# A fused attention and feed-forward layer: the weighted sums of four heads issued in two bursts instead of five units

## The chip, the cores and the metric

One core of one Trainium2 chip. The metric is the device time of one execution in microseconds (us), as the median of several runs. The kernel works in float32, except for the score products, whose operands are split into three bfloat16 levels each.

## What is computed

For 8 batches of 512 tokens with 128 features: attention with 16 heads of width 8, added to the input and normalised, then a feed-forward part with a shift by one token, added and normalised again. Cut to what matters:

```python
raw = einsum('bhid,bhjd->bhij', q, k)
scores = alpha * tanh(raw / beta) + lam * hamming + lat      # two rank-6 biases, made from x
scores = where(causal, scores, -inf)
attn = softmax(scores)
out = einsum('bhij,bhjd->bhid', attn, v) @ out_w.T
x = layernorm(x + out)
x = layernorm(x + sigmoid(xr @ W_r.T) * (square(relu(xk @ W_k.T)) @ W_v.T))
```

## The kernel before, in words

The scores of a head are kept transposed, keys on the partitions and queries along the free side. Keys come in four blocks of 128 (jb 0 to 3), and block jb needs only the queries from 128·jb on, because of the causal mask. Four heads make a **quad**; its 16 blocks are packed into 5 **pairs** of two 512-wide banks: pairs 0 and 1 of a quad hold block 0 of two heads each, pairs 2 and 3 hold blocks 1 and 3 (384 and 128 wide) of two heads each, pair 4 holds block 2 (256 wide) of all four. So a batch is 4 quads, or 20 pairs (`PAIRS`), and the whole kernel is a pipeline over pairs.

A pair t goes through the engines like this. TensorE makes the products q·k into one of three PSUM slots (`scores`, tile `raw<-q_stack,k_stack`), and a slot is free again when VectorE has read it. ScalarE takes the tanh (L783, `raw` to `probs`). TensorE overwrites the slot with the biases (`biases`, `raw<-i_stack,j_stack`). VectorE adds both (`main`, L1004). ScalarE takes the exponential in place (L788), GpSimd zeroes the masked triangle (`mask`, L892), and TensorE multiplies by the values into the single PSUM bank `sums` (`weighted`). `probs` has ten pair buffers, and tanh of a pair waits until the weighted sums of the pair ten earlier have been counted by `pv_done`. Two quads accumulate in `sums`; then VectorE copies it out (`sums_out`, L1067) before the next quad may start.

All engines run one list of **steps**, t = 0 to 19 for each batch b, in program order, with fixed lags: in step t TensorE issues biases of pair t-1 and scores of pair t+1, ScalarE tanh of pair t and exp of pair t-3, VectorE `main` of t-1, GpSimd the mask of t-3. Beside them each step carries **side work** from fixed tables. Before attention of a batch can start its operands are prepared two batches ahead ("prep" for b+2), after it its output is finished one batch behind ("post" for b-1):

- TensorE: the tables `PREP_UNITS`, `VALUES_UNITS`, `POST_UNITS`. Every such unit writes the one PSUM bank `side_bank`, and each waits until the unit before it was read (`Side.before`). Prep: xT2 (transposes), q2, k2, F2, G2 (projections). Values: v1. Post: oT0, oT1 (transposes of `sums_sb`), aT, y, x1T, kk, rr, kv.
- VectorE: `PREP` and `POST`. Splitting a 512-wide float32 matrix into three bfloat16 levels alternates between engines: `hi` (VectorE, L1038), `rest` (GpSimd, L899), `mid` (VectorE, L1043), `lo` (GpSimd, L905). `mid` waits for `rest` of the same matrix (Q, K, J or G), and `rest` waits for `hi`. `values_in` (L1055) copies v1 out of `side_bank`. `residual` (L1101), `stats` (L1089) and `moments` (L1096) follow the unit y.
- GpSimd: `PREP` and `POST`: `inv_std` (L913, L915) and `norm` (L923, L927) make the normalised x1, which the unit x1T transposes.
- ScalarE: F2, kk and rr are read there (L796; L798 with L804; L800).

SyncE writes the levels to DRAM and loads them back as stacks (`q_stack`, `k_stack`, `i_stack`, `j_stack`) for the batch after.

`VALUES_STEPS` gives each of the 20 weighted units its step; a step of 20 or more is step minus 20 of the next batch. Unit p of a quad is: p = 0 and 1 the two halves (256 wide) of block 0, p = 2 block 1 (384), p = 3 block 3 (128), p = 4 block 2 (256); each is four products, one per head, in four column groups of the array. `AHEAD_FIRST` names the steps in which TensorE issues the scores of t+1 before the side units rather than last. Inside a step of TensorE the order is biases, (scores), side units, weighted sums left from the batch before, weighted sums of this batch, (scores).

Batch 0 has no post work; batches 1 to 5 have both; batch 6 has no prep but v1; batch 7 has neither, and a tail follows in which the last weighted sums and the last post work run by themselves.

Of the kernel before, what the change touches and what calls it, by code (L numbers as in the profile page):

```python
# [42 lines left out]
P = 128  # L43
# [18 lines left out]
VALUES_STEPS = [6, 7, 7, 9, 11, 11, 12, 13, 14, 15, 16, 18, 19, 19, 19, 20, 20, 24, 25, 25]  # L62
# [6 lines left out]
VALUES_UNITS = {7: ["v1"]}  # L69
POST_UNITS = {1: ["oT0"], 6: ["oT1"], 8: ["aT"], 10: ["y"], 14: ["x1T"], 16: ["kk"], 17: ["rr"], 18: ["kv"]}  # L70
# [69 lines left out]
def build(nc, x, qkv_w, out_w, hex_w, lam_logit, q6_w, transforms, transform_weights, scale_logit,  # L140
# [17 lines left out]
    with ExitStack() as ctx:  # L158
# [350 lines left out]
        def _(pe):  # L509
# [47 lines left out]
            def weighted(b, par, t):  # L557


                quad, p = divmod(t, PAIRS_PER_QUAD)  # L560
                k, s = divmod(quad, 2)

                pe.wait_ge(mask_done, PAIRS * b + last_of_group(t) + 1)
                if t == 0:
                    pe.wait_ge(dve_freed, side_units.made(b, "v"))
                if t == PAIRS // 2 or (t == 0 and not (isinstance(b, int) and b == 0)):
                    pe.wait_ge(sums_read, 2 * b + k)
                first_pair = last_of_group(t) - (1 if p < 4 else 0)

                def head(r, a, z):  # L570

                    return pair_probs(first_pair + (r // 2 if p < 4 else 0))[:, r % 2 if p < 4 else r // 2, a:z]


                jb, first, cols_of = [
                    (0, 0, lambda r: head(r, 0, T // 2)), (0, T // 2, lambda r: head(r, T // 2, T)),
                    (1, P, lambda r: head(r, 0, 3 * P)), (3, 3 * P, lambda r: head(r, 3 * P, T)),
                    (2, 2 * P, lambda r: head(r, (r % 2) * 2 * P, (r % 2 + 1) * 2 * P))][p]
                for r in range(4):
                    rhs = cols_of(r)  # L580
                    last = mm(sums[32 * r:32 * r + 32, first:first + rhs.shape[-1]],
                              values[par][:, jb, 4 * quad + r, :], rhs, start=(s == 0 and p == 0),
                              stop=(s == 1 and p == PAIRS_PER_QUAD - 1), skip_group_check=True)
                last.then_inc(pv_done, 1)
# [67 lines left out]
            def values_of(b, par, step):  # L652

                for t in range(PAIRS):
                    if VALUES_STEPS[t] == step:
                        weighted(b, par, t)
# [703 lines left out]
```

## Time and profile before

| | |
|---|---|
| median of 3 runs | 427.74 us (426.52 to 428.01) |
| the profiled execution | 426.69 us, span 424.7 us |
| TensorE products busy | 368.2 us, 87% |
| VectorE busy | 328.3 us, 77% |
| ScalarE busy | 327.3 us, 77% |
| GpSimd busy | 230.1 us, 54% |
| tanh and exp (L783, L788) | 160 each, mean 1025 and 1060 ns |
| main (L1004) | 160, mean 1273 ns |
| mean granted TensorE clock | 0.949 of full |

Busy time counts from start to end of each instruction; neighbours on one engine overlap by some hundredths of a microsecond, so that the distance from start to start is a little shorter than the duration. A product in float32 leaves two records in the trace, so four heads of one weighted unit are 8 records (1280 in all for 640 products). In the timeline, a number in brackets is the time for which the engine sat idle before, and what ended it.

### The profile page before, as it was taken

Reading aid. Unit: us, or ns where it says so; the run is one execution under the profiler, and the core shown is the slowest. Engines: PE = TensorE matmul, PEld = TensorE weight load, DVE = VectorE, ACT = ScalarE, POOL = GpSimd, SP = SyncE. Lnnn points to the kernel's source line nnn. Section 1 sums busy time; section 2 is a strip of 40 time slices with the busy share of each in tenths; the row PEclk is TensorE's granted clock in tenths of the full one; section 3 lists DMA queues with packets and bytes.
Section 4 is the critical chain, followed back from the end, with each engine's and each line's share of the span. In section 5 each row is a group of like instructions: output and inputs, shape, how many; then the busy total and the mean of one; then the engine's idle time right before and its main releaser. Section 6 shows DMA issues by size and latency. Waiting matters only on the chain.

```text
span 424.7 us, 8760 instructions
## 1 busy us (share of the span) xinstructions
PE 368.2 (87%) x2907; PEld 190.1 (45%) x2907; DVE 328.3 (77%) x539; ACT 327.3 (77%) x364; POOL 230.1 (54%) x367
## 2 busy tenths in 40 slices
PE   3557688899999999999899989999999998999863
PEld 1132233345455444645464446444544454345453
DVE  4874668987978788778978897879878867696643
ACT  1102398998998988798889899898889998999621
POOL 4313535823687449633975388645873446344631
PEclk9955899999999999999999999999999999899958
DMA  3254587786622774166634763376318620100000
GB/s 97 87 152 119 157 261 195 215 230 175 197 91 59 192 198 160 48 176 183 173 88 120 188 185 106 90 187 185 114 50 208 165 79 1 51 26 1 2 26 25
DMA packets 37807, 53.74 MB, mean 127 GB/s; under 512 B 3522, under 2 KB 35266, under 8 KB 36190
## 3 DMA queue, kind: packets, MB, share of 16 engines
q1 hardware_dynamic: 34078, 51.49, 43.4%
q10 hardware_dynamic: 3696, 1.84, 1.7%
q8 instruction: 18, 0.29, 0.3%
q14 instruction: 15, 0.12, 0.1%
HBM read 38.69 MB, written 14.61 MB: 126 GB/s over the span
## 4 chain that ended last, share of the span: by engine, by line
PE 43%; DVE 19%; issue 11%; POOL 10%; SPq 7%; ACT 5%; DMA 3%; ACTq 1%; DVEq 0%; POOLq 0%
PE raw L511 17%; PE side_bank L511 13%; PE sums L511 10%; DVE probs L1004 9%; ACT probs L788 3%; POOL probs L892 2%; ACT probs L783 2%; SPq L401 2%; PE side_bank L598 2%; POOL x L927 2%; POOL x L923 2%; SPq L415 2%; POOL parts L905 2%; SPq L412 2%; DVE bn L1089 1%
## 5 line engine op out<-in xcount | busy, mean ns | idle before, releaser
L1004 DVE SCALAR_TENSOR_TENSOR probs<-probs,scal,raw 128x1024 f32<-128x1024 f32 x160 | 202.3, 1273 | 32.5 <-PE raw L511 32.0
L783 ACT ACTIVATE probs<-raw 128x1024 f32<-128x1024 f32 x160 | 163.9, 1025 | 38.4 <-PE raw L511 37.7
L892 POOL TENSOR_SCALAR_AFFINE_SELECT probs<-probs 128x256 f32<-128x256 f32 (+1 forms) x224 | 98.5, 457 | 137.3 <-ACT probs L788 136.8
L788 ACT ACTIVATE probs<-probs 128x1024 f32<-128x1024 f32 x160 | 169.3, 1060 | 0.9 <-DVE probs L1004 0.9
L511 PE MATMUL raw<-q_stack,k_stack 72*128 72x384 bf16 (+3 forms) x512 | 98.2, 304 | 17.3 <-DVE probs L1004 13.6
L511 PE MATMUL raw<-i_stack,j_stack 111*128 111x384 bf16 (+3 forms) x512 | 97.2, 302 | 2.4 <-ACT probs L783 2.3
L511 PE MATMUL sums<-probs,values 128*32 128x256 f32 (+2 forms) x1280 | 93.4, 392 | 4.2 <-POOL probs L892 4.0
L511 PEld LDWEIGHTS raw<-q_stack,k_stack 72*128 72x128 bf16 x512 | 38.1, 98 | 71.4 <-DVE probs L1004 46.9
L511 PEld LDWEIGHTS raw<-i_stack,j_stack 111*128 111x128 bf16 x512 | 42.2, 98 | 47.4 <-issue 16.9
L511 PEld LDWEIGHTS sums<-probs,values 128*32 128x32 f32 x1280 | 29.7, 109 | 50.0 <-issue 26.1
L899 POOL TENSOR_TENSOR whole<-whole,parts 128x512 f32<-128x512 f32 x22 | 26.1, 1188 | 23.5 <-DVE parts L1038 23.5
L905 POOL TENSOR_TENSOR parts<-whole,parts 128x512 bf16<-128x512 f32 x30 | 35.1, 1170 | 4.2 <-DVE parts L1043 4.2
L1067 DVE COPY sums_sb<-sums 128x512 f32<-128x512 f32 x15 | 10.4, 692 | 20.0 <-PE sums L511 20.0
L1043 DVE CAST parts<-whole 128x512 bf16<-128x512 f32 x32 | 16.7, 522 | 2.9 <-POOL whole L899 2.8
L915 POOL TENSOR_TENSOR rstd<-var_eps,minus_half 128x4 f32<-128x4 f32 x14 | 14.6, 1046 | 1.2
L796 ACT ACTIVATE feats<-side_bank 128x512 f32<-128x512 f32 x8 | 4.9, 612 | 12.4 <-PE side_bank L511 12.4
L511 PEld LDWEIGHTS side_bank<-w_r_mix,x1T 128*128 128x128 f32 x112 | 13.6, 191 | 1.0
L511 PE MATMUL side_bank<-w_r_mix,x1T 128*128 128x128 f32 x112 | 13.6, 275 | 0.0
L1038 DVE CAST parts<-whole 128x512 bf16<-128x512 f32 x24 | 11.9, 498 | 1.8 <-DMA q_rows<-parts 1.6
L511 PE MATMUL side_bank<-x1T,w_k_mix 128*128 128x512 f32 x28 | 13.2, 591 | 0.0
L835 ACT ACTIVATE probs<-shift_col 1x1536 bf16<-1x1536 bf16 x1 | 1.5, 1481 | 14.6 <-DVE w_r_mix L1244 14.6
L1089 DVE BATCH_NORM_STATS2 bn<-res 128x6 f32<-128x128 f32 x56 | 12.2, 280 | 0.2
(144 smaller groups left out, 346.4 us busy)
## 6 DMA issues: line engine op xcount, KB each, us to landing
q_stack<-q_rows SPq DMA_DIRECT2D x21, 384.0 KB
k_stack<-k_rows SPq DMA_DIRECT2D x21, 384.0 KB
i_stack<-lattice_i SPq DMA_DIRECT2D x21, 288.0 KB
i_stack<-hamming_i SPq DMA_DIRECT2D x21, 288.0 KB
q_rows<-parts SPq DMA_DIRECT2D x8, 384.0 KB, 8.5
k_rows<-parts SPq DMA_DIRECT2D x8, 384.0 KB, 2.6
lattice_i<-parts SPq DMA_DIRECT2D x8, 288.0 KB
k_rows<-parts SPq DMA_DIRECT2D x8, 256.0 KB, 3.0
```

Of the source, the lines that this page charges most:

```text
L511: return nc.tensor.matmul(o, lhsT, rhs, start=start, stop=stop, **kw)
L783: nc.scalar.activation(pair_probs(t), raw[:, t % PSUM_PAIRS, :].rearrange("p (u i) -> p u i", u=2), ACT.Tanh).then_inc(tanh_done, 1)
L788: nc.scalar.activation(pair_probs(t), pair_probs(t), ACT.Exp).then_inc(exp_done, 1)
L892: last = nc.gpsimd.affine_select(out=v, in_=v, compare_op=ALU.is_ge, fill=0.0, base=0, pattern=[[0, v.shape[1]], [1, P]], channel_multipli ...
L899: nc.gpsimd.tensor_tensor(whole[:, kind, :], feats[:] if kind == J else whole[:, kind, :], parts[:, kind, 0, :], ALU.subtract).then_inc(re ...
L905: nc.gpsimd.tensor_tensor(parts[:, kind, 2, :], whole[:, kind, :], parts[:, kind, 1, :], ALU.subtract).then_inc(lo_done[kind], 1)
L915: nc.gpsimd.tensor_tensor(rstd[:], var_eps[:], minus_half[:], ALU.pow).then_inc(rstd_done, 1)
L1004: v.scalar_tensor_tensor(out=o, in0=o, scalar=scal[:, 2:3], in1=raw[:, t % PSUM_PAIRS, :].rearrange("p (u i) -> p u i", u=2), op0=ALU.mult ...
L1038: v.tensor_copy(parts[:, kind, 0, :], feats[:] if kind == J else whole[:, kind, :]).then_inc(hi_done[kind], 1)
L1043: v.tensor_copy(parts[:, kind, 1, :], whole[:, kind, :]).then_inc(mid_done[kind], 1)
L1067: v.tensor_copy(sums_sb[:, k, :], sums[:]).then_inc(sums_read, 1)
L1089: v.bn_stats(bn[:, blk, :], res[:, blk, :]).then_inc(bn_done, 1)
```

## The change

The five weighted units of a quad become two bursts. Part 0 multiplies block 0 of the four heads in full width (512) when pairs 0 and 1 are masked, and counts 2 on `pv_done`; part 1 multiplies blocks 1, 3 and 2 when all five pairs are masked, and counts 3. The steps are (6, 9), (11, 14), (16, 19), (21, 24), so 8 bursts per batch in place of 14 groups of adjacent units. The unit v1 and `values_in` move from step 7 to 11. The unit y, `residual`, `stats` and `moments` of the first normalisation move from 10 to 9, GpSimd's `inv_std` from 10 to 9 and its `norm` from 11 to 10. The unit kk (and ScalarE's part) moves from 16 to 15. On VectorE `hi` of Q moves from 5 to 4, `mid` of Q from 9 to 8, `hi` of K from 9 to 10, and `sums_out` comes after `main` of its step instead of ahead of it (in steps 5 and 15).

```diff
-VALUES_STEPS = [6, 7, 7, 9, 11, 11, 12, 13, 14, 15, 16, 18, 19, 19, 19, 20, 20, 24, 25, 25]
+VALUES_STEPS = [(6, 9), (11, 14), (16, 19), (21, 24)]
-VALUES_UNITS = {7: ["v1"]}
-POST_UNITS = {1: ["oT0"], 6: ["oT1"], 8: ["aT"], 10: ["y"], 14: ["x1T"], 16: ["kk"], 17: ["rr"], 18: ["kv"]}
+VALUES_UNITS = {11: ["v1"]}
+POST_UNITS = {1: ["oT0"], 6: ["oT1"], 8: ["aT"], 9: ["y"], 14: ["x1T"], 15: ["kk"], 17: ["rr"], 18: ["kv"]}
...
-            def weighted(b, par, t):
+            def weighted(b, par, quad, part):
+                pairs = (2, 3)[part]
+                pe.wait_ge(mask_done, PAIRS * b + first_pair + (2 if part == 0 else PAIRS_PER_QUAD))
...
+                blocks = [[(0, lambda r: head(r // 2, r % 2, 0, T))],
+                          [(1, lambda r: head(2 + r // 2, r % 2, 0, 3 * P)),
+                           (3, lambda r: head(2 + r // 2, r % 2, 3 * P, T)),
+                           (2, lambda r: head(4, r // 2, (r % 2) * 2 * P, (r % 2 + 1) * 2 * P))]][part]
+                for jb, cols_of in blocks:
+                    for r in range(4):
+                        last = mm(sums[32 * r:32 * r + 32, jb * P:T], values[par][:, jb, 4 * quad + r, :], cols_of(r),
+                                  start=(s == 0 and part == 0), stop=(s == 1 and jb == 2), skip_group_check=True)
+                last.then_inc(pv_done, pairs)
...
 (GpSimd)
-            POST = {10: [(inv_std, 0)], 11: [(norm, 0)], 18: [(gated_residual,)], 19: [(inv_std, 1), (norm, 1)]}
+            POST = {9: [(inv_std, 0)], 10: [(norm, 0)], 18: [(gated_residual,)], 19: [(inv_std, 1), (norm, 1)]}
...
 (VectorE)
-            PREP = {0: [(x_out,)], 2: [(projected, Q)], 3: [(projected, K)], 5: [(hi, Q)], 9: [(mid, Q), (hi, K)],
+            PREP = {0: [(x_out,)], 2: [(projected, Q)], 3: [(projected, K)], 4: [(hi, Q)], 8: [(mid, Q)], 10: [(hi, K)],
                     11: [(mid, K), (hi, J)], 12: [(features_i,)], 13: [(hi, G)], 15: [(mid, J)], 17: [(mid, G)]}
-                    10: [(residual,), (stats, 0, 0), (stats, 0, 1), (moments, 0)], 14: [(x1_out,)],
+                    9: [(residual,), (stats, 0, 0), (stats, 0, 1), (moments, 0)], 14: [(x1_out,)],
...
-                    if t == VALUES_STEPS[-1] - PAIRS and post:
-                        sums_out(b - 1, 1)
-                    if t == VALUES_STEPS[PAIRS // 2 - 1]:
-                        sums_out(b, 0)
                     if t >= BIAS_LAG or post:
                         main(*lagged(b, t, BIAS_LAG))
+                    if t - 1 == VALUES_STEPS[-1][1] - PAIRS and post:
+                        sums_out(b - 1, 1)
+                    if t - 1 == VALUES_STEPS[QUADS // 2 - 1][1]:
+                        sums_out(b, 0)
```

## Rows read from the trace of the kernel before

**Rows 1.** Busy us of PE, PEld, DVE, ACT, POOL; clock, DMA share, GB/s: one period.

```profile
181.80:227.20 45.40, 43.09 (x362) 22.60 (x360) 38.47 (x61) 40.25 (x45) 28.68 (x45) 1.00 0.53 145
```

**Rows 2.** Waits from 181.8 to 227.2 us: total, times, longest (us).

```profile
ACT probs L783 <- PE raw L511: 4.9, 8, 1.5
...
DVE sums_sb L1067 <- PE sums L511: 2.7, 2, 2.0
```

**Rows 3.** Timeline, ScalarE: tanh of pair 2 in batches 3 and 4.

```profile
181.41 1.01 ACT L783 ACTIVATE probs<-raw 128x1024 f32<-128x1024 f32 x1
...
226.82 1.02 ACT L783 ACTIVATE probs<-raw 128x1024 f32<-128x1024 f32 x1
```

**Rows 4.** Timeline, TensorE: groups of weighted units and what came next.

```profile
200.81 1.07 PE L511 MATMUL sums<-probs,values 128*32 128x256 f32 x16
...
201.81 0.61 PE L511 MATMUL raw<-q_stack,k_stack 72*128 72x384 bf16 x4
...
220.38 1.50 PE L511 MATMUL sums<-probs,values 128*32 128x384 f32 x24
...
221.83 0.60 PE L511 MATMUL raw<-q_stack,k_stack 72*128 72x512 bf16 x2
```

**Rows 5.** Timeline, VectorE: the copy of the sums in step 5.

```profile
189.13 0.69 DVE L1067 COPY sums_sb<-sums 128x512 f32<-128x512 f32 x1 [2.00 <-PE sums L511]
```

**Rows 6.** Timeline, steps 7 to 13 of batch 3: side work and the tanh of pair 13.

```profile
194.52 0.76 DVE L1055 COPY values<-side_bank 128x256 f32<-128x256 f32 x2
...
198.95 1.06 PE L511 MATMUL side_bank<-woT,attnT 128*128 128x128 f32 x8
...
201.34 0.68 DVE L1101 TENSOR_TENSOR res<-side_bank,x_res 128x512 f32<-128x512 f32 x1
...
201.88 1.17 POOL L905 TENSOR_TENSOR parts<-whole,parts 128x512 bf16<-128x512 f32 x1
...
202.69 1.02 PE L511 MATMUL side_bank<-feats,lat_map 128*128 128x512 f32 x2
...
203.00 1.17 POOL L899 TENSOR_TENSOR whole<-whole,parts 128x512 f32<-128x512 f32 x1
203.07 0.38 DVE L1096 BATCH_NORM_AGGREGATE mean_var<-bn 128x2 f32<-128x6 f32 x4 [0.15 <-DVE bn L1089]
...
203.37 1.26 DVE L1004 SCALAR_TENSOR_TENSOR probs<-probs,scal,raw 128x1024 f32<-128x1024 f32 x1
...
203.64 0.64 PE L511 MATMUL sums<-probs,values 128*32 128x256 f32 x8
204.14 0.23 POOL L913 TENSOR_SCALAR var_eps<-mean_var 128x4 f32<-128x4 f32 x1
204.44 1.05 POOL L915 TENSOR_TENSOR rstd<-var_eps,minus_half 128x4 f32<-128x4 f32 x1
204.55 0.42 DVE L1043 CAST parts<-whole 128x512 bf16<-128x512 f32 x1
...
205.33 1.02 ACT L783 ACTIVATE probs<-raw 128x1024 f32<-128x1024 f32 x1 [0.63 <-PE raw L511]
205.46 0.77 POOL L892 TENSOR_SCALAR_AFFINE_SELECT probs<-probs 128x256 f32<-128x256 f32 x2
```

**Rows 7.** Busy time by stretch, 364 to 366 us, batch 7, and the same columns.

```profile
364.00:366.00 2.00, 2.00 (x12) 0.59 (x12) 1.01 (x1) 2.00 (x3) 0.42 (x2) 0.51 0.03 8
```

**Rows 8.** Timeline, ScalarE and TensorE: tanh of pairs 4 to 6 of batches 6 and 7.

```profile
321.29 1.03 ACT L783 ACTIVATE probs<-raw 128x1024 f32<-128x1024 f32 x1
...
324.99 1.05 ACT L783 ACTIVATE probs<-raw 128x1024 f32<-128x1024 f32 x1
...
363.85 1.03 ACT L783 ACTIVATE probs<-raw 128x1024 f32<-128x1024 f32 x1
...
368.35 1.02 ACT L783 ACTIVATE probs<-raw 128x1024 f32<-128x1024 f32 x1 [0.66 <-PE raw L511]
```

**Rows 9.** Timeline, TensorE: the last weighted unit of the kernel.

```profile
401.94 0.64 PE L511 MATMUL sums<-probs,values 128*32 128x256 f32 x8 [0.76 <-POOL probs L892]
```

More of the change, by code:

```diff
@@ L555, in biases @@
                 last.then_inc(bias_ready, 1)
-            def weighted(b, par, t):
-                quad, p = divmod(t, PAIRS_PER_QUAD)
+            def weighted(b, par, quad, part):
                 k, s = divmod(quad, 2)
-                pe.wait_ge(mask_done, PAIRS * b + last_of_group(t) + 1)
-                if t == 0:
+                first_pair = PAIRS_PER_QUAD * quad
+                pairs = (2, 3)[part]
+                pe.wait_ge(mask_done, PAIRS * b + first_pair + (2 if part == 0 else PAIRS_PER_QUAD))
+                if quad == 0 and part == 0:
@@ L565, in weighted @@
                     pe.wait_ge(dve_freed, side_units.made(b, "v"))
-                if t == PAIRS // 2 or (t == 0 and not (isinstance(b, int) and b == 0)):
+                if s == 0 and part == 0 and not (quad == 0 and isinstance(b, int) and b == 0):
                     pe.wait_ge(sums_read, 2 * b + k)
-                first_pair = last_of_group(t) - (1 if p < 4 else 0)
-                def head(r, a, z):
-                    return pair_probs(first_pair + (r // 2 if p < 4 else 0))[:, r % 2 if p < 4 else r // 2, a:z]
@@ L575, in weighted @@
[L575 to L583, printed above, removed]
@@ L584, in weighted, with head @@
-                last.then_inc(pv_done, 1)
+                def head(pair, unit, a, z):
+                    return pair_probs(first_pair + pair)[:, unit, a:z]
+                blocks = [[(0, lambda r: head(r // 2, r % 2, 0, T))],
[6 more added lines that the diff above has]
+                                  start=(s == 0 and part == 0), stop=(s == 1 and jb == 2), skip_group_check=True)
@@ L652, in values_of @@
             def values_of(b, par, step):
-                for t in range(PAIRS):
-                    if VALUES_STEPS[t] == step:
-                        weighted(b, par, t)
+                for quad, steps in enumerate(VALUES_STEPS):
+                    if step in steps:
+                        weighted(b, par, quad, steps.index(step))
             parity = [1]
@@ L738, in _ @@
                        range(JB)).then_inc(tail["first_sums_T"], 1)
-            for step in range(PAIRS, VALUES_STEPS[-1] + 1):
+            for step in range(PAIRS, VALUES_STEPS[-1][1] + 1):
                 values_of(B - 1, 1, step)
```

## The prediction, made before the changed kernel was run

> **What bounds the kernel now.** I read the page first, then busy time by stretch, the waits of one period, and the timeline step by step. One batch in the steady state is a period of 45.4 us, from one tanh of pair 2 to the next [rows 3]. No engine fills it: in that stretch TensorE is busy 43.1 us, ScalarE 40.3 and VectorE 38.5 [rows 1]. All three hand the same pair on, so the period is the work of ScalarE plus the time for which it waits for scores. That wait is 4.9 us in 8 places, at most 1.5 in one [rows 2]; some 40.5 us is the floor. Every side task is to be judged by whether it makes a tanh start later. The profiled execution has 426.69 us, 1.05 below the median of 427.74; I sum differences and add them to the median.
>
> **The change part by part.**
>
> *Bursts.* Two units of 256 take 1.00 us to the start of what follows, three of 384, 128 and 256 together take 1.45 [rows 4]. So 256 columns cost 0.45 and each burst about 0.1 more. Entering a burst is not seen apart; I bound both sides together by 0.1 and 0.25 us. Per batch 6 of 14 entries go: 0.6 to 1.5 us of TensorE. The 512-wide product is in no row; the nearest is the 1.00 for the same columns, which I take, between 0.9 and 1.1. What this gives by itself is nothing unless TensorE is what a tanh waits for; it also makes each remaining block longer (1.45 us), and what is queued behind it, the biases or scores of the next pair, waits for that. The Trainium skill (TensorEngine Tiling (Array Packing), Key Properties) says that changing the tiling mode drains the engine, which speaks for the change; the rows agree in that a burst costs more than its columns. By that rule alone each batch would gain its 1.5 us.
>
> *Copies of the sums.* Before, VectorE stood 2.0 us ahead of the copy in step 5, `main` of pair 4 behind it [rows 5], of 2.7 us in a period [rows 2]. Afterwards `main` goes first. `main` is no longer held, but the copy ends later, and oT1 waits for it on TensorE, with the first burst and the scores of pair 7 queued behind.
>
> *Steps 4 to 9.* I walked the queues from tanh of pair 2 at 181.41, with scores or biases 0.44 us apart, 0.64 from a product group's start to its reader, exp 0.91 after tanh and the next tanh 0.94 after exp (estimates from neighbours in the timeline). The burst in step 4 ends at 187.5, `main` of pair 4 runs from 188.1 to 189.4, the copy to 190.0, oT1 at 190.0, the first burst from 190.6 to 191.6. Tanh of pair 6 keeps its place, that of pair 7 is 0.4 late. Without v1 and two units in step 7, tanh of pair 9 comes at 196.0, 1.2 us earlier than before. y can start at 196.2, when aT has been copied (before: 198.95 [rows 6]); residual follows 1.06 later at 197.3, and moments end at 199.4, where they ended at 203.45 before [rows 6].
>
> *Steps 10 to 12, the term that decides.* Let m be the end of moments. GpSimd stands at `inv_std` in step 9, so in its queue follow inv_std 1.32 (204.14 to 205.46), the mask of pair 7 0.77, lo of Q 1.12 and rest of K 1.17 [rows 6], with about 0.2 to wake: rest of K is done at m + 4.6. Before, lo and rest ran while the moments were being made and inv_std stood behind them, so `mid` of K found its input ready. VectorE after m has `main` of 9 and 10 (1.18 each, 203.37 to 204.55) and hi of K (0.4 to 0.6): it is at `mid` of K at m + 2.9 and stops for 1.7 us. Behind that stop are mid of K and hi of J (0.33 each), and now values_in (0.76), which used to be in step 7 [rows 6]: done at m + 6.1. TensorE's G2 may not write the bank before v1 is out of it, G2 takes 0.95 (202.69 to 203.64), and in step 12 the scores of pair 13 stand behind G2: tanh of pair 13 at m + 7.7, 207.1 to 207.2. Before: 205.33 [rows 6]. TensorE stands 2.6 us ahead of G2. Loss at this point: 1.8 us, where without the stop it would be 0.1. Ends for the stop: nothing, if y or moments come so late that GpSimd does lo and rest first in effect; 2.6, all of TensorE's wait.
>
> *Steps 13 to 2.* The norm ends 2 us earlier than it did but now x1T no longer is what is late. kk in step 15 has x1T ready; ScalarE's relu and square come one pair earlier, same work. mid, hi and gate keep their places relative to the pair. The burst of quad 3 moves from step 0 to step 1 of the next batch, from ahead of scores 1 to ahead of scores 2; scores 1 waits for `main` of 19 anyway, which stands behind the second statistics. So the burst, hidden under that wait before, now costs: 0.5 us, against savings of about 0.6 before it. The walk ends with tanh of pair 2 at 228.5 against 226.82 [rows 3]: a period of 47.1, +1.7.
>
> *The sum.* Five periods have prep and post: 5 x 1.7 = 8.5. Batch 6 has no mid of K, but v1 and a burst in step 11 and the burst in step 1: +1.1 by the same walk. Batch 0 has no moments; its hi of Q, a step earlier, waits for the same transfer with `main` of 4 behind it, won back by step 9: +0.7 with its end. Batch 7: 0. Tail: after the last mask came one unit of 256, 0.64 [rows 9]; now comes the whole part 1, 1.49 in all: +0.85. Together 11.1, less rounding 11.0: 427.7 + 11.0 = **438.7 us**.
>
> *SyncE* gets its levels in the same order, some 2 us later for Q and K; their readers are a batch away, so nothing. Masks wait at most for inv_std; the earliest reader of a late one is the burst in step 14, done with it 2 us ahead. `pv_done` comes in lumps, three or more steps ahead of the tanh that needs it: nothing.
>
> **Rivals.** (a) *Faster: TensorE's entries are what bounds.* If TensorE's queue is the limit, 1.5 us go for each of 7.5 batches: 416.5. For it: 43.1 busy of 45.4, and 2.7 us of VectorE's waits that vanish. Against it: the walk finds G2 waiting for a copy, not for TensorE. It decides if rest of K is done by m + 2.9. Chance 0.18, spread from 415 to 425.
> (b) *No change.* The stop is there but covered: tanh of pairs 11 and 12 late from other causes, so that 13 loses nothing more, as the walk without the stop has it. 427 to 429. Chance 0.12.
> (c) *Slower still, by the clock.* In 364 to 366 the granted clock was 0.51, the level of 1.2 GHz [rows 7], after a sparse stretch of TensorE; tanh 4 to tanh 6 took 4.50 us there against 3.70 in batch 6 [rows 8]. A stop of 2.6 us ahead of G2 in five periods could call it each time: 5 x 0.8 = 4 more, 443. The Trainium skill (TensorE: Matmul & The Clock Gate, What's actually happening) says that the throttled state is the default and activity releases it; by that the gap could only harm. Against it: gaps of 0.4 to 1 us in the steady periods left the clock at 1.00 [rows 1]. Chance 0.12.
>
> **How the numbers follow.** Forecast 0.58 (433 to 441.5). A measurement tells about 0.5% from no change, so same is 425.6 to 429.9. Slower 0.70 (forecast and c), same 0.12, faster 0.18. The range from 427 to 444 leaves out rival (a), nearly all of it, and a little above. The likeliest case alone: 433 to 441.5, from the stop's 1.2 to 2.0 us in five periods and the burst's 0.1 us in 56 bursts.
>
> **What would show it.** Tanh of pair 2 some 47 us apart; five idle times of 1.2 to 2 us of VectorE ahead of L1043, ended by GpSimd's L899; TensorE waiting over 2 us for VectorE's L1055 ahead of the unit G2; ScalarE's wait for scores grown from 4.9 to nearly 7 us a period; the 2.0 us ahead of L1067 gone. If L1043 shows no such wait, or tanh of pair 13 comes within 24.5 us of that of pair 2 (before 23.9), I am wrong at steps 10 to 12. If the wait is there and the period has not grown, I am wrong in what it costs.

## The result, and the profile of the changed kernel

| | before | changed |
|---|---|---|
| median on one chip | 427.16 us (4 runs) | 467.38 us (4 runs, 465.01 to 469.01) |
| ratio | | 1.0926, 95% interval 1.0876 to 1.0975 |
| the profiled execution | 426.69 us, span 424.7 us | 467.9 us, span 466.0 us |
| TensorE's mean granted clock | 0.949 | 0.932 |

Medians are over all runs of a kernel; ratios leave out those more than 1.5% above its fastest (four of ten in e14, three of ten in e15, none elsewhere).

The sign of the forecast was right and its size was not: 40 us were lost, not 11, and the time lies above the range. The first look is at the busy time of the page of the changed kernel, since it tells whether work was added or waiting.

```profile
PE 378.4 (81%) x2651; PEld 196.6 (42%) x2651; DVE 344.4 (74%) x539; ACT 327.5 (70%) x364; POOL 230.3 (49%) x367
```

ScalarE and GpSimd work as long as before (327 and 230 us), so on them the 41 us of span are waiting. TensorE has 256 product records less but 10 us more busy time, and VectorE 16 us more with the same number of instructions: something makes single instructions longer. The groups by line name which (busy us, mean ns | idle time before them and what ended it).

```profile
L781 ACT ACTIVATE probs<-raw 128x1024 f32<-128x1024 f32 x160 | 163.6, 1023 | 77.1 <-PE raw L511 76.4
...
L1041 DVE CAST parts<-whole 128x512 bf16<-128x512 f32 x32 | 25.6, 800 | 10.6 <-POOL whole L897 10.4
L511 PE MATMUL side_bank<-feats,lat_map 128*128 128x512 f32 x16 | 15.3, 1056 | 23.8 <-DVE values L1053 22.6
```

The same groups before the change:

```profile
L783 ACT ACTIVATE probs<-raw 128x1024 f32<-128x1024 f32 x160 | 163.9, 1025 | 38.4 <-PE raw L511 37.7
...
L1043 DVE CAST parts<-whole 128x512 bf16<-128x512 f32 x32 | 16.7, 522 | 2.9 <-POOL whole L899 2.8
L511 PE MATMUL side_bank<-feats,lat_map 128*128 128x512 f32 x16 | 10.1, 720 | 1.2 <-DVE lat_map L1198 1.2
```

Line numbers in this region have gone down by two. ScalarE's wait for scores went from 37.7 to 76.4 us: those 38.7 us are nearly the whole loss, on the engine that hands every pair on. G2 waits 22.6 us for `values_in` where it waited for nothing, and `mid` waits 10.4 us for `rest` (before 2.8); both waits were forecast. Not forecast are the means: the cast of `mid` went from 522 to 800 ns, G2 from 720 to 1056 ns.

One period, from the tanh of pair 2 in batch 3 to that in batch 4, is 52.08 us where [rows 1] and [rows 3] have 45.4. Its stretch (same columns as [rows 1]) and then its waits:

```profile
198.91:250.99 52.08, 45.06 (x339) 23.91 (x338) 42.84 (x62) 42.23 (x47) 29.23 (x45) 0.97 0.47 127
```

```profile
ACT probs L781 <- PE raw L511: 11.5, 8, 5.5
...
PE side_bank L511 <- DVE values L1053: 4.3, 1, 4.3
...
DVE parts L1041 <- POOL whole L897: 1.9, 1, 1.9
```

The number of waits for scores is still 8, as in [rows 2], but one of them alone has 5.5 us, more than all eight together in [rows 2]. The timeline of steps 10 to 13 of batch 3 shows how it is built; it answers to [rows 6].

```profile
216.89 0.38 DVE L1094 BATCH_NORM_AGGREGATE mean_var<-bn 128x2 f32<-128x6 f32 x4 [0.15 <-DVE bn L1087]
...
218.36 0.42 DVE L1036 CAST parts<-whole 128x512 bf16<-128x512 f32 x1
...
220.65 1.15 POOL L897 TENSOR_TENSOR whole<-whole,parts 128x512 f32<-128x512 f32 x1
...
221.76 1.04 POOL L921 TENSOR_TENSOR x<-res,mean_var 128x512 f32<-128x512 f32 x1
221.84 1.25 DVE L1041 CAST parts<-whole 128x512 bf16<-128x512 f32 x1 [1.87 <-POOL whole L897]
222.95 1.04 POOL L925 TENSOR_TENSOR x<-x,rstd 128x512 f32<-128x512 f32 x1
223.01 1.26 DVE L1036 CAST parts<-feats 128x512 bf16<-128x512 f32 x1
...
224.19 0.74 DVE L1053 COPY values<-side_bank 128x256 f32<-128x256 f32 x2
...
224.99 1.90 PE L511 MATMUL side_bank<-feats,lat_map 128*128 128x512 f32 x2 [4.28 <-DVE values L1053]
...
226.68 1.06 PE L511 MATMUL raw<-q_stack,k_stack 72*128 72x384 bf16 x4
...
227.78 1.02 ACT L781 ACTIVATE probs<-raw 128x1024 f32<-128x1024 f32 x1 [5.50 <-PE raw L511]
```

Moments end at 217.27 (216.89 and 0.38). `rest` of K ends at 221.80 (220.65 and 1.15), 4.5 us later (forecast 4.6), and VectorE stands for 1.87 us ahead of `mid` of K (forecast 1.7). Up to here the walk holds to a tenth. Then two things happen that it did not have. The casts `mid` of K and `hi` of J take 1.25 and 1.26 us instead of 0.42: each begins within 0.1 us of a GpSimd operation of the norm (L921, L925) and ends 0.28 us after it. And TensorE, after 4.28 us of standing, does G2 in 1.90 us and the scores behind it in 1.06, about twice their time. The granted clock tells why (columns as before).

```profile
221.00:223.00 2.00, 0.00 (x0) 0.00 (x0) 1.17 (x1) 1.28 (x2) 1.85 (x3) 1.00 0.96 288
...
225.00:227.00 2.00, 2.00 (x3) 0.61 (x4) 1.20 (x2) 0.00 (x0) 0.49 (x1) 0.55 0.43 139
```

It is 1.00 as the gap begins and 0.55 behind it, close to the level of 1.2 GHz. So tanh of pair 13 comes 10.5 us after the end of moments, where 7.7 was forecast.

The loss stretch by stretch, from the issue of the load `x_res` in one batch to that in the next (SyncE's timeline):

| stretch | before | changed | lost | forecast |
|---|---|---|---|---|
| start to batch 1 | 86.4 | 89.0 | 2.6 | 0.7 |
| batches 1 to 5 | 231.8 | 262.6 | 30.8 | 8.5 |
| batch 6 | 42.6 | 46.3 | 3.7 | 1.1 |
| batch 7 and tail | 63.9 | 68.1 | 4.2 | 0.85 |

Each of the five full periods lost 4.7 to 7.0 us instead of 1.7. (The two mean clocks in the table at the top can't be held against each other for this: the profiled execution of the kernel before stood at about half clock from 20 to 44 us, ahead of batch 1, the changed kernel's did not; between 54 and 364 us the kernel before had 1.00 throughout, while the changed one had about half in eight stretches between 61 and 355 us.)

### The profile page after: what moved, and what is told of

Read it like the earlier page. It is cut to its first block, busy times and chain, and to the rows that moved or that the text cites. A ratio compares the mean times of both kernels' runs of the same rounds, so it can differ in the third digit from the quotient of the medians.

```text
span 466.0 us, 8246 instructions
## 1 busy us (share of the span) xinstructions
PE 378.4 (81%) x2651; PEld 196.6 (42%) x2651; DVE 344.4 (74%) x539; ACT 327.5 (70%) x364; POOL 230.3 (49%) x367
## 4 chain that ended last, share of the span: by engine, by line
PE 40%; ACT 16%; DVE 15%; issue 12%; POOL 6%; SPq 6%; DMA 3%; DVEq 0%; POOLq 0%; ACTq 0%
PE raw L511 18%; PE sums L511 10%; PE side_bank L511 9%; ACT probs L781 8%; ACT probs L786 7%; DVE probs L1002 3%; PE side_bank L596 3%; DVE parts L1036 2%; DVE bn L1087 2%; SPq L401 2%; POOL res L931 2%; SPq L415 1%; POOL whole L897 1%; SPq L412 1%; POOL probs L890 1%
## 5 line engine op out<-in xcount | busy, mean ns | idle before, releaser
L781 ACT ACTIVATE probs<-raw 128x1024 f32<-128x1024 f32 x160 | 163.6, 1023 | 77.1 <-PE raw L511 76.4
L511 PE MATMUL raw<-q_stack,k_stack 72*128 72x384 bf16 (+3 forms) x512 | 104.6, 320 | 20.5 <-DVE probs L1002 18.0
L511 PE MATMUL raw<-i_stack,j_stack 111*128 111x384 bf16 (+3 forms) x512 | 103.4, 317 | 8.8 <-ACT probs L781 8.6
L511 PE MATMUL sums<-probs,values 128*32 128x512 f32 (+3 forms) x1024 | 87.7, 463 | 3.7 <-POOL probs L890 2.8
L511 PEld LDWEIGHTS raw<-q_stack,k_stack 72*128 72x128 bf16 x512 | 43.7, 103 | 90.7 <-issue 40.5
L511 PEld LDWEIGHTS raw<-i_stack,j_stack 111*128 111x128 bf16 x512 | 44.0, 103 | 52.9 <-ACT probs L781 19.7
L511 PEld LDWEIGHTS sums<-probs,values 128*32 128x32 f32 x1024 | 26.6, 113 | 34.7 <-issue 23.3
L511 PE MATMUL side_bank<-feats,lat_map 128*128 128x512 f32 x16 | 15.3, 1056 | 23.8 <-DVE values L1053 22.6
L1041 DVE CAST parts<-whole 128x512 bf16<-128x512 f32 x32 | 25.6, 800 | 10.6 <-POOL whole L897 10.4
L913 POOL TENSOR_TENSOR rstd<-var_eps,minus_half 128x4 f32<-128x4 f32 x14 | 14.6, 1046 | 1.2
L511 PEld LDWEIGHTS side_bank<-feats,lat_map 128*128 128x128 f32 x16 | 3.5, 270 | 27.7 <-DVE values L1053 25.6
L1036 DVE CAST parts<-whole 128x512 bf16<-128x512 f32 x24 | 10.6, 441 | 4.1 <-DMA q_rows<-parts 3.9
L794 ACT ACTIVATE feats<-side_bank 128x512 f32<-128x512 f32 x8 | 4.8, 600 | 12.5 <-PE side_bank L511 12.4
```

The costliest lines, as they stand in the source:

```text
L511: return nc.tensor.matmul(o, lhsT, rhs, start=start, stop=stop, **kw)
L781: nc.scalar.activation(pair_probs(t), raw[:, t % PSUM_PAIRS, :].rearrange("p (u i) -> p u i", u=2), ACT.Tanh).then_inc(tanh_done, 1)
L913: nc.gpsimd.tensor_tensor(rstd[:], var_eps[:], minus_half[:], ALU.pow).then_inc(rstd_done, 1)
L1036: v.tensor_copy(parts[:, kind, 0, :], feats[:] if kind == J else whole[:, kind, :]).then_inc(hi_done[kind], 1)
L1041: v.tensor_copy(parts[:, kind, 1, :], whole[:, kind, :]).then_inc(mid_done[kind], 1)
```

## The experiments

Sixteen kernels were run, each beside the kernel before on the same chip (its median there was 426.4 to 427.8 us). "Changed +" means that the edit is made to the changed kernel, "before +" to the kernel before.

| label | kernel | median us | ratio to before (95%) |
|---|---|---|---|
| e1_v7 | changed + v1 back at 7 | 459.6 | 1.076 (1.064 to 1.087) |
| e2_inv10 | changed + inv_std, norm back at 10, 11 | 447.6 | 1.048 (1.031 to 1.065) |
| e3_norm11 | changed + norm alone back at 11 | 457.8 | 1.072 (1.058 to 1.086) |
| e4_fill | changed + zero-weight products in the gaps | 453.7 | 1.062 (1.044 to 1.080) |
| e5_v7_inv10 | e1 and e2 together | 447.8 | 1.052 (1.047 to 1.056) |
| e6_bursts_only | bursts and copies; all side work as before | 448.3 | 1.052 (1.047 to 1.056) |
| e7_sides_only | before + all of the side work's moves | 473.0 | 1.111 (1.106 to 1.116) |
| e8_v7_inv10_q20 | e5 + burst of quad 3 at 20 | 443.4 | 1.041 (1.036 to 1.046) |
| e9_bursts_s15first | e6 + scores of 15 ahead of x1T | 438.6 | 1.028 (1.023 to 1.033) |
| e10_bursts_s15_q20 | e9 + burst of quad 3 at 20 | 433.9 | 1.017 (1.012 to 1.023) |
| e11_before_s15first | before + scores of 15 ahead of x1T | 425.4 | 0.997 (0.994 to 0.999) |
| e12_before_copy_behind | before + copies of sums behind `main` | 421.0 | 0.987 (0.983 to 0.991) |
| e13_copy_behind_s15first | e11 and e12 together | 421.1 | 0.983 (0.979 to 0.987) |
| e14_e10_split_wait | e10 + block 2 alone waits for the fifth mask | 433.5 | 1.008 (1.004 to 1.012) |
| e15_before_v11 | before + v1 at 11 | 430.2 | 1.005 (1.001 to 1.008) |
| e16_sides_v7 | e7 with v1 left at 7 | 462.4 | 1.081 (1.075 to 1.087) |

### The chain at steps 10 to 12

Either the chain GpSimd, VectorE, G2 with stretched casts and the clock is the whole loss, or a part of it lies elsewhere, in the bursts. Three kernels cut one link each; each expectation says what its own letters stand for.

```diff
 e1_v7
-VALUES_UNITS = {11: ["v1"]}
+VALUES_UNITS = {7: ["v1"]}
 e2_inv10
-            POST = {9: [(inv_std, 0)], 10: [(norm, 0)], 18: ...
+            POST = {10: [(inv_std, 0)], 11: [(norm, 0)], 18: ...
 e3_norm11
-            POST = {9: [(inv_std, 0)], 10: [(norm, 0)], 18: ...
+            POST = {9: [(inv_std, 0)], 11: [(norm, 0)], 18: ...
```

> The changed kernel (467.4 us, a period of 52.1 against 45.4) with v1 and its copy back in step 7. Theory A, that the loss comes of G2 waiting for the copy of v1 behind mid of K: TensorE's wait of 4.3 us ahead of G2 goes in all five steady periods, and with it the fall of the clock in step 12; about 4 us a period, so 447 us, although VectorE still stands 1.9 us ahead of mid of K. Theory B, that VectorE's stop and its slow casts cost by themselves, since main of pair 11 stands behind them too: 460 or more. Theory C, that the loss lies in the bursts: no change, 465 to 469.

> The changed kernel with inv_std back in step 10 and norm in step 11 of GpSimd. Theory A or B, that GpSimd's order stops mid of K: no wait of VectorE ahead of mid of K, casts back to 0.42 us, G2's wait down to under 1 us; about 5 us a period, 442 us. Theory C, bursts or the burst at the turn of the batch: 465 or more.

> The changed kernel with only norm moved back to step 11, inv_std stays in step 9. GpSimd's rest of K ends as late as before, so VectorE still waits some 1.9 us ahead of mid of K, but no norm runs beside the casts. If the casts of 1.25 us were held up by the norm on GpSimd: both at 0.42 us, 1.7 us less in each of five periods, about 459 us. If the casts are slow for another reason (DMA, the wait itself): still 1.25 us and 467.

**e1** (-7.8 us: the 460 of a stop that costs by itself, not the 447 of G2's wait alone): G2 no longer waits for `values_in`, its mean is 727 ns, but VectorE still stands ahead of `mid` for 11.8 us in all and the two casts stay at 1.25 and 1.27. **e2** (-19.8 us, where 442 had been expected) is the strongest single return. The stop at `mid` of K is gone and `mid` of K and `hi` of J are short again (`hi` of K, now beside `lo`, takes 1.31), yet G2 waits for `values_in`, 10.9 us in 6 places. Its timeline at the same place:

```profile
213.04 0.44 DVE L1041 CAST parts<-whole 128x512 bf16<-128x512 f32 x1
...
213.28 1.09 POOL L913 TENSOR_TENSOR rstd<-var_eps,minus_half 128x4 f32<-128x4 f32 x1
213.40 0.41 DVE L1036 CAST parts<-feats 128x512 bf16<-128x512 f32 x1
213.73 0.74 DVE L1053 COPY values<-side_bank 128x256 f32<-128x256 f32 x2
...
214.53 1.96 PE L511 MATMUL side_bank<-feats,lat_map 128*128 128x512 f32 x2 [1.72 <-DVE values L1053]
...
215.09 1.04 POOL L921 TENSOR_TENSOR x<-res,mean_var 128x512 f32<-128x512 f32 x1
```

Read the GpSimd rows: beside its operation on 4 columns (L913) the cast takes 0.41; the norm (L921) now comes when the casts are over. And G2 takes 1.96 us after a gap of only 1.72, at a granted clock of 0.54. This looks as if v1 at 11 did harm even where `rest` is in time; e5, below, shows that taking it back gives nothing here.

**e3** moves the norm alone, the wait for moments staying at step 9. It gives back 9.6 us while the stop ahead of `mid` is still there (12.4 us in all); what has changed are the casts, in batch 3 and by the groups:

```profile
220.16 0.61 DVE L1041 CAST parts<-whole 128x512 bf16<-128x512 f32 x1 [1.87 <-POOL whole L897]
...
222.03 1.12 PE L511 MATMUL side_bank<-feats,lat_map 128*128 128x512 f32 x2 [2.99 <-DVE values L1053]
```

```profile
L1036 DVE CAST parts<-feats 128x512 bf16<-128x512 f32 x8 | 5.6, 694 | 2.0 <-ACT feats L794 2.0
```

In the changed kernel that last group (`hi` of J) has a mean of 1098 ns and 8.8 us in all, and all `mid` together 25.6 us against 22.2 here. The casts are thus 6.6 us shorter, most of the 9.6, as far as moving the norm touches nothing else. They don't come down to the 0.42 that was expected: `mid` of K now runs beside two masks of GpSimd and takes 0.61.

### The clock's share

```diff
+                    if t == 12 and post and prep:
+                        fill(18)
                     for use in units_at(t, post, prep, values):
                         side(b, use)
+                    if t == 0 and post and prep:
+                        fill(7)
```

`fill(n)` issues n products of 512 columns with zero weights into `sums`, ahead of G2 and ahead of scores 1, in the five full batches: they add zero to the sums.

> The changed kernel with idle time of TensorE filled: 18 products of 512 columns with zero weights into the open bank of sums ahead of G2 in step 12, 7 ahead of the scores in step 0, batches with prep and post. Nothing waits less; only the clock can change. Clock theory: G2 back from 1.9 to 1.02 us, the burst in step 1 from 1.72 to 1.07, granted clock 1.00 in both places, 2.5 us a period, about 455 us. If the clock is no part of the loss, or the filling delays what it stands before: 467 to 475.

```profile
215.11 4.05 PE L514 MATMUL sums<-filler,zeros 128*128 128x512 bf16 x18
...
219.55 1.12 PE L514 MATMUL side_bank<-feats,lat_map 128*128 128x512 f32 x2 [0.40 <-DVE values L1068]
...
220.51 0.60 PE L514 MATMUL raw<-q_stack,k_stack 72*128 72x384 bf16 x4
```

Work was added and 13.7 us went (11.0 and 16.4 in the two runs there are, so the interval of the ratio is wide). `values_in` ends as late as before, 7.7 us behind moments; the gap is only filled, and G2 and the scores run at full speed (clock 1.00 from 219 to 223). From 71 to 336 us, nearly all of the five filled periods, the clock was 1.00 throughout. In the profiled execution these five together took 250.6 us instead of 262.6. Idle products take no wait away, so 11 to 16 of the 40 us are what TensorE's clock costs behind the gaps, 2.4 to 2.7 us for each of five periods, the turn of the batch included; the forecast had 0.8 for it, in a rival with a chance of 0.12.

### Side work alone, bursts alone

```diff
 e6_bursts_only (on the changed kernel)
-VALUES_UNITS = {11: ["v1"]}
+VALUES_UNITS = {7: ["v1"]}
-POST_UNITS = {..., 9: ["y"], 14: ["x1T"], 15: ["kk"], ...}
+POST_UNITS = {..., 10: ["y"], 14: ["x1T"], 16: ["kk"], ...}
 (VectorE's and GpSimd's tables likewise as before)
```

e7 makes all these moves, and no other, on the kernel before; e16 is e7 with v1 left at 7; e15 moves v1 alone; e5 returns v1 and GpSimd's two entries to the changed kernel and leaves the other moves.

> The changed kernel with both returned: v1 and its copy in step 7, inv_std in step 10 and norm in step 11. If the two are separate causes of one stop (with inv_std back alone the kernel took 447.6 us, and TensorE still stood 1.7 us ahead of G2, with a fall of the clock behind it): no wait ahead of G2, no clock below 1.00 in steps 12 and 13, 2.3 us a period less, 436 us. If what is left in that kernel lies in the bursts and in the turn of the batch: 443 to 448.

> Only the bursts and the copies of the sums behind main; all side work placed as in the kernel before. If the side work made the loss: within 427 to 433 us, the rest being the burst of quad 3 in step 1 (0.5 us a period) and 0.85 us in the tail; TensorE saves 6 entries a batch. If the bursts are the loss: 445 or more.

> The other half: the five units in their old steps and the copies of the sums ahead of main, all side work placed as in the changed kernel. If the side work made the loss: 450 to 467 us, with VectorE waiting 1.9 us ahead of mid of K, casts of 1.25 us, and TensorE standing 4 us ahead of G2. If it takes the bursts as well: 440 or less.

> The kernel before with only v1 and its copy moved from step 7 to 11. Its rest of K is done in time, so VectorE does not wait at mid of K, but values_in still follows main of 10, mid of K and hi of J, and G2 waits for it. Theory A needs both moves: G2's wait about 2 us, with a fall of the clock, 2.5 us a period, less what step 7 gives back (1.5 us): 427 to 437 us. If the place of v1 alone made the loss of the side work: 455 or more. If it is free: 425 or less.

> The kernel before with all side moves of the change except v1, which stays in step 7. VectorE waits ahead of mid of K and its casts stand under the norm (3.5 us together), but TensorE's G2 no longer waits for it; only main of pair 11 does. If the loss needs both moves (the stop, and a unit of TensorE that stands on its end): 430 to 440 us. If the stop costs the same by itself through main of 11: 455 or more.

Both halves of the change lose by themselves: side work +46.6 us (e7), bursts with the copies behind `main` +21.9 (e6). Together they lose 40, less than the sum, so they share waits. e5 and e6 are equal, so the moves of y, kk, `hi` and `mid` of Q and `hi` of K cost nothing once the bursts are there. e5 also equals e2 (447.8 and 447.6), where 436 had been expected: with GpSimd's order taken back, taking v1 back as well gives nothing. The timeline of e5 shows why:

```profile
216.41 1.08 PE L596 MATMUL side_bank<-ident,x 128*128 128x128 f32 x4 [1.36 <-POOL x L925]
...
220.39 1.02 ACT L781 ACTIVATE probs<-raw 128x1024 f32<-128x1024 f32 x1 [3.57 <-PE raw L511]
```

G2's waits for `values_in` (10.9 us in e2) are gone, but now x1T waits for the norm (6.8 us, in e2 nothing), and instead of tanh of pair 13 (3.00 us in e2) that of pair 15 stands, for 3.57 us. One gap has taken the place of the other. So beside the bursts GpSimd's early order alone is all of the side work's loss. Without bursts v1 by itself costs 2 to 3 us (e15, by the ratio and by the median), some 11 on top of the other moves (e7 against e16), and those others, GpSimd's order among them, about 35 (e16), a part of it for a reason that the forecast had denied. The timeline of e16:

```profile
221.60 1.25 DVE L1043 CAST parts<-whole 128x512 bf16<-128x512 f32 x1 [1.87 <-POOL whole L899]
...
223.71 1.91 POOL L892 TENSOR_SCALAR_AFFINE_SELECT probs<-probs 128x256 f32<-128x256 f32 x4
...
224.72 1.51 PE L511 MATMUL sums<-probs,values 128*32 128x384 f32 x8 [3.00 <-POOL probs L892]
...
226.16 1.03 PE L511 MATMUL raw<-q_stack,k_stack 72*128 72x256 bf16 x4
...
227.23 1.02 ACT L783 ACTIVATE probs<-raw 128x1024 f32<-128x1024 f32 x1 [3.95 <-PE raw L511]
```

GpSimd makes the masks behind inv_std, lo, rest and the whole norm, and a weighted unit in step 13 stands 3.00 us for one of them; the scores behind it come at half speed and late. Over the kernel the sums wait 19.2 us for masks in e16 and 4.0 before. In e7, where v1 makes TensorE wait ahead of G2 first, it is 4.0 again. With bursts, step 13 has no reader of a mask, and the changed kernel doesn't show this wait (2.8 us over the kernel, all in the tail).

### What the bursts cost

```diff
 e9_bursts_s15first (on e6), e11_before_s15first (on the kernel before)
-AHEAD_FIRST = [2, 3, 4, 7, 9, 18]
+AHEAD_FIRST = [2, 3, 4, 7, 9, 14, 18]
 e8_v7_inv10_q20 (on e5), e10_bursts_s15_q20 (on e9)
-VALUES_STEPS = [(6, 9), (11, 14), (16, 19), (21, 24)]
+VALUES_STEPS = [(6, 9), (11, 14), (16, 19), (20, 24)]
```

> v1 in step 7, inv_std in 10, norm in 11, and the first burst of quad 3 in step 0 of the next batch (as the units it came from) rather than step 1. The prediction had the burst hidden in step 0 under the wait of scores 1 for main of pair 19, and costing 0.5 us in step 1: 3 to 4 us less than the same kernel with it in step 1. If the place makes nothing: the same within 1 us. If the burst in step 0 holds back scores 1: slower.

> The kernel with the bursts alone (448.3 us), and step 14 added to the steps in which TensorE issues the scores first. Theory D: the bursts cost because what used to fill TensorE's idle time in steps 12 and 13 now stands behind x1T, which waits for the norm, and ahead of scores 15; ScalarE's 2.6 us ahead of tanh 15 should go, biases of 14 still wait, so 1.5 to 2 us a batch with post work, 434 to 438 us. Rival E, that the loss lies at the turn of the batch and in the tail: 446 to 448.

> The same, and the first burst of quad 3 in step 0 instead of 1. This place gave 4.4 us with the side work nearly as before (447.8 to 443.4). If D and the place are separate: 430 to 434 us. If bursts are harmless wherever nothing stands behind them, it comes within 1 percent of the kernel before, the rest being the tail (nearly 3 us).

> The kernel before with the scores of step 14 first, five units as they were. Its tanh 15 waits 0.44 us only. If D is right the gain here is small: 424 to 427 us. If scores first in step 14 is good by itself, whatever the bursts: 418 or less, and the gain of the run with bursts says nothing of them.

The timeline of e6 in steps 13 and 14, all side work being where it was before:

```profile
213.15 1.04 POOL L925 TENSOR_TENSOR x<-x,rstd 128x512 f32<-128x512 f32 x1
...
214.33 0.63 PE L596 MATMUL side_bank<-ident,x 128*128 128x128 f32 x4 [1.36 <-POOL x L925]
...
215.03 1.50 PE L511 MATMUL sums<-probs,values 128*32 128x384 f32 x24
...
216.46 0.60 PE L511 MATMUL raw<-q_stack,k_stack 72*128 72x512 bf16 x2
...
217.10 1.02 ACT L781 ACTIVATE probs<-raw 128x1024 f32<-128x1024 f32 x1 [2.57 <-PE raw L511]
```

Before, TensorE did a unit of 384 columns in step 13 while the norm was being made, and only one of 128 stood between x1T and the scores of pair 15. Now it has none while it waits (1.36 us), and then the whole burst of 1.43 us stands ahead of the scores: tanh of 15 waits 2.57 us, where the kernel before had 0.44. Putting those scores ahead of x1T gives 9.7 us back (e9) with bursts and 1.9 without (e11), so it is the burst that made them late, in a kernel whose side work is where it was. In the changed kernel, which was not run with this edit, tanh of pair 15 waits only 0.39 us in batch 3: there all of TensorE is late from G2 on, and x1T waits for nothing. The burst of quad 3 at step 20 gives 4.4 (e8) and 4.7 us (e10): ahead of scores 1 it is hidden, as the forecast said, but its price at step 21 is 0.6 to 0.7 us in each of seven periods, not 0.5 less what the earlier bursts save. Together these take the bursts' loss from 21.9 to 6.6 us.

What is left was looked for in the last burst, which waits for all five masks:

```diff
-                pe.wait_ge(mask_done, ... + (2 if part == 0 else PAIRS_PER_QUAD))
+                pe.wait_ge(mask_done, ... + (2 if part == 0 else 4))
...
+                    if jb == 2:
+                        pe.wait_ge(mask_done, ... + PAIRS_PER_QUAD)
```

> The kernel with bursts, scores first in step 14 and quad 3 in step 0 (433.9 us), with the wait inside part 1 split: blocks 1 and 3 start when four masks are done, block 2 waits for the fifth. In the tail TensorE stood 2.8 us ahead of a burst of 1.5 us; blocks 1 and 3 (1.0 us) come forward out of it: 1 us less there. In the steady periods masks are done long before, nothing. If the one wait were the rest of the loss, 427 to 429; if only the tail, 432 to 433.

The tail of e10, then of e14:

```profile
406.08 1.50 PE L511 MATMUL sums<-probs,values 128*32 128x384 f32 x24 [2.80 <-POOL probs L890]
...
407.64 0.76 DVE L1306 COPY sums_sb<-sums 128x256 f32<-128x256 f32 x2 [2.79 <-PE sums L511]
```

```profile
406.68 1.07 PE L511 MATMUL sums<-probs,values 128*32 128x384 f32 x16 [1.17 <-POOL probs L892]
408.32 0.64 PE L511 MATMUL sums<-probs,values 128*32 128x256 f32 x8 [0.56 <-POOL probs L892]
```

Two thirds of the burst now lie ahead of the last mask, as meant, and VectorE's copy of the sums waits 1.92 us for the end of it, not 2.79: 0.9 us of the tail. The median hardly moved (433.9 and 433.5), and its runs spread from 428.0 to 435.9 us. It may be worth those 0.9 us; more can't be read from this.

### The copies of the sums

```diff
-                    if t == VALUES_STEPS[-1] - PAIRS and post:
-                        sums_out(b - 1, 1)
-                    if t == VALUES_STEPS[PAIRS // 2 - 1]:
-                        sums_out(b, 0)
                     if t >= BIAS_LAG or post:
                         main(*lagged(b, t, BIAS_LAG))
+                    if t == VALUES_STEPS[-1] - PAIRS and post:
+                        sums_out(b - 1, 1)
+                    if t == VALUES_STEPS[PAIRS // 2 - 1]:
+                        sums_out(b, 0)
```

> The kernel before with the two copies of sums behind main of their step. The prediction has main no longer held for 2.0 us in step 5 and oT1 waiting instead: within 2 us of before, 425 to 429. If the 2.0 us bounded the period: 7 x 1 to 1.5 us less, 418 us.

> The kernel before with both small changes: the copies behind main, and the scores first in step 14. If their gains (6.3 us and 1.9 us) are of different waits they add: 418 to 420 us. If the one takes the place of the other: 421 us.

This is the one part of the change that gains, and it beats both kernels: **421.0 us**, ratio 0.987. VectorE in step 5 of batch 3, to be held against [rows 5]:

```profile
187.17 1.28 DVE L1004 SCALAR_TENSOR_TENSOR probs<-probs,scal,raw 128x1024 f32<-128x1024 f32 x1 [0.32 <-PE raw L511]
...
188.85 0.69 DVE L1067 COPY sums_sb<-sums 128x512 f32<-128x512 f32 x1 [0.40 <-PE sums L511]
```

Counted from tanh of pair 2 (181.12 here, 181.41 in [rows 3]), `main` of pair 4 begins 6.1 us later where it was 8.3, and the copy 7.7 us later in both: the copy comes no later for letting `main` go first. VectorE's waits for sums fell from 20.0 us to 2.0 over the kernel, and tanh of pair 9 waits 0.55 us where it waited 1.53. 425 to 429 had been expected, from a forecast that gave this part no gain of its own. e13 adds the other small gain and gets the same median, so the two do not clearly add up.

## Why the prediction was right or wrong

**Bursts (the durations: right).** The 512-wide block takes 1.00 us and part 1 takes 1.43 to 1.45, as in [rows 4]. The saving of up to 1.5 us of TensorE per batch was never seen in the time. The Trainium skill (TensorEngine Tiling (Array Packing), Key Properties) says that a change of the tiling mode drains the engine; the traces agree in so far as a burst costs 0.1 us more than its columns, but don't show the drain apart. The 2.57 us for which tanh of pair 15 stands in e6 are more than the 0.6 to 1.5 that the forecast hoped to save.

**Steps 4 to 9 (right), copies of the sums (gain not seen).** The walk had tanh of pair 9 at 14.6 us after that of pair 2, and it came at 14.6 (213.50 less 198.91), where it was 15.8 before. But it put this down to v1 and the units of step 7 alone. Of the copies it said "Main is no longer held, but the copy ends later": by itself that move ends the copy no later and brings tanh of pair 9 from 15.8 to 14.7 us, and gains 6.3 us over the kernel (e12). I had [rows 5] before me and priced only the chain behind the copy, not the one behind `main`.

**Steps 10 to 12 (mechanism right, sized too low).** Every named wait is there: the stops ahead of `mid` of K (10.4 us in 6 places, the longest 1.9), G2 behind `values_in`, tanh of pair 13 at 28.9 us after that of pair 2, beyond the 24.5 that I had set as the bound. Two terms were missing. "mid of K and hi of J (0.33 each)" took 1.25 and 1.26, since the norm, moved by the same change, now runs beside them; and G2 "0.95" took 1.90 with the scores behind it at 1.06, by the clock. So `values_in` ended 7.7 us after moments instead of 6.1, and tanh of 13 came at 10.5 instead of 7.7. This is the step that failed first and most: "Loss at this point: 1.8 us" was 5.0 (28.9 us from tanh of pair 2 to that of pair 13, before 23.9). e3 (-9.6 us) measures the first of the two, in the main, and e4 (-13.7, with the turn of the batch) the second.

**The clock (rival c: right in kind, wrong in weight and size).** It was an alternative to the forecast with a chance of 0.12 and 0.8 us a period. In truth it was a part of the forecast: whoever forecasts that TensorE stands for 2.6 us ahead of G2 has to price what comes behind it. It measured 2.4 to 2.7 us a period, with the turn of the batch (e4).

**"x1T no longer is what is late" (true of the changed kernel, and no saving).** The norm does end 2 us earlier in the period, and x1T waits for nothing (before 3.2 us in all); but it is TensorE that is late by then, behind G2. What I missed is the other thing a burst does: it takes away the unit with which TensorE passed the time until x1T and puts it ahead of the scores. With the side work in its old place that is the largest part that was found of the bursts' 21.9 us (9.7 by e9); in the changed kernel it lies hidden behind G2, and comes out as soon as G2's wait is taken away (e5). The forecast never looked for it. The burst of quad 3, "0.5 us, against savings of about 0.6 before it", cost 4.4 to 4.7 us over the kernel (e8, e10).

**Masks "2 us ahead" (true for bursts only).** In the changed kernel none is waited for in step 13; with five units a late one costs 3.0 us (e16).

**Tail.** From the tail's first transposes to its copy of the sums it is 7.46 us where it was 4.63, +2.8 against +0.85: the last burst of three blocks ran at about half clock (2.79 us instead of 1.50; granted 0.56 from 440 to 442), after waiting 2.80 us for its mask. In e10 the same burst after the same wait took 1.50 at 1.00, so this part can come or not. [rows 9] had shown a unit at full clock behind a wait of 0.76.

**Rivals (a) and (b)** fell: no period got shorter, and the stop was not covered. The end on the faster side had 0.18 and rested in part on VectorE's waits that vanish; they did vanish, and alone are worth the 6.3 us of e12.

**The sum.** Five periods of 1.7 against 6.2 measured is 22 of the 30 us by which the forecast of the span was short. The others are the head (+1.9), batch 6 (+2.6) and batch 7 with the tail (+3.4).

**What stays open.** The last 6 us or so of the bursts' loss (e10, e14) have no proven cause; the clock falls in some of their periods. What decides whether a gap lowers the clock wasn't found, and its length alone does not: at the turn of batch 3 the clock went to 0.50 after a gap of 1.80 us, at the turn of batch 4 it stayed at 1.00 after one of 1.43; after 1.36 us ahead of x1T it was low in e5 (x1T took 1.08) and not in e6 (0.63); in e2 G2 took 1.13, 1.70, 1.96, 1.80 and 1.51 us in the five periods, after gaps of 1.62 to 1.72; and after 2.99 us ahead of G2 it held in e3 (G2 took 1.12), and fell 1 to 2 us later with TensorE at work. The scores first in step 14 were not tried on the changed kernel. Bursts with the copies still ahead of `main` weren't run, so how much of e6's loss the copies already hide isn't known.

## What to carry to other kernels

Small units of work in an in-order queue are not overhead alone: those that lie between two waits fill the time until the second, so before bunching them look at what the engine would do in that time and at what stands behind the bunch. When a wait is taken away, look which one was hidden behind it: here the next gap took the whole gain (e5 against e2). When one engine's operation is moved, price also the instructions that will now run beside it on others, and treat a forecast gap of TensorE as possibly two costs, the gap and the slower clock behind it. And take each part of a change for itself: here two copies put behind `main` were the only part that gained, and the forecast had set them at nothing.

## What the runs showed of the hardware

- **A VectorE cast is held by a GpSimd operation beside it.** A cast of 128x512 from float32 to bfloat16 takes 0.42 us alone and 1.25 to 1.26 when a GpSimd operation on 128x512 has begun 0.06 to 0.08 us before; it ends 0.28 to 0.29 us after that. The Trainium skill (SBUF — State Buffer, Who interferes with whom) says that the two engines share a port pair that a copy or cast in a two-port mode contends for, and that the one that issues first holds it for its whole instruction while the other is blocked. The traces agree (in e3, where the norm's first operation begins 0.31 us after the cast, it is that operation that takes longer, 1.20 us instead of 1.04), with one exception: beside GpSimd's operation on 4 columns, which is as long (1.05 to 1.09 us), the cast took 0.41 to 0.42 ([rows 6] at 204.55, and e2), so there the length of the other instruction was not what held it.
- **TensorE's clock can be at half behind gaps of under 2 us.** G2 took 1.96 us after a gap of 1.72 (e2, granted 0.54), with the clock at 1.00 up to its start; scores and transposes at the turn of batch 3 ran at 0.50 of full clock after 1.80 us. Other gaps as long or longer left it at 1.00 for the work right behind them (2.99 us in e3, 2.80 in the tail of e10). The Trainium skill (TensorE: Matmul & The Clock Gate, Why this matters for your kernels) bids one keep TensorE free of idle gaps between matmuls above a certain length; these two were shorter than the length that it names, so here the measurement goes further than the page.
- **Idle products can pay.** 18 products with zero weights (4.05 us) in one gap and 7 in another kept the clock at 1.00 in five periods, and the kernel became 13.7 us faster for them (e4, two runs, 11.0 and 16.4).
